# Attention and mixture of experts on one core: the last scatter moved ahead of an adding load, five statistics half a block later, the first output store ahead of a wait

## The reference, cut to what matters

```python
x = x + layernorm(attn(layernorm(x)))            # x is [8, 512, 256] f32: 8 batches of 512 tokens
# the second half, on flat = layernorm(x) as 4096 tokens of 256:
probs = softmax(flat @ gate_W); topk_w, topk_idx = top_k(probs, 2)      # 8 experts, 2 for each token
out = 0.5 * gelu(flat @ shared_W + shared_b)
for e in range(8):
    out = out + combine[:, e:e+1] * (gelu(flat @ W1[e] + b1[e]) @ W2[e] + b2[e])
out = layernorm(out) * gamma + beta              # the inner norm, then gamma and beta
x = x + layernorm(out)                           # the outer norm, then the residual
```

## Time and profile before

| | |
|---|---|
| median of three runs | 739.98 us (738.08 to 740.19) |
| profiled execution | 744.36 us |
| its span in the trace | 742.6 us |
| TensorE matmul busy | 610.8 us, 82% |
| VectorE busy | 447.2 us, 60% |
| ScalarE busy | 448.9 us, 60% |
| GpSimd busy | 278.4 us, 37% |
| mean granted TensorE clock | 0.937 |

### The profile page before, as it was taken

The page is one execution under the profiler, slowest core; times in us unless marked ns, Lnnn a source line. Parts: engine busy times, 40 slices in busy tenths (PEclk is TensorE's granted clock), DMA queues, the critical chain, the costliest instruction groups (busy, mean ns, idle before and its releaser), DMA issues. The chain is left out here.

```text
span 742.6 us, 16982 instructions
## 1 busy us (share of the span) xinstructions
PE 610.8 (82%) x5031; PEld 519.4 (70%) x5031; DVE 447.2 (60%) x1247; ACT 448.9 (60%) x887; POOL 278.4 (37%) x381
## 2 busy tenths in 40 slices
PE   4778887787776898977979989999999999999400
PEld 3667676576665687855858877889989988888300
DVE  4479898898986554422437533344444445768757
ACT  2557756756744665533734765767666654687755
POOL 4000333443437322644762422334334455352131
PEclk9889999999998899988999999999999999999755
DMA  7453654551265221202112311122212149552378
GB/s 256 173 208 128 194 181 133 153 171 58 78 199 180 73 87 58 59 30 59 59 30 59 104 42 59 43 75 86 73 45 60 48 96 195 120 93 53 71 156 169
DMA packets 45272, 78.25 MB, mean 105 GB/s; under 512 B 16962, under 2 KB 30596, under 8 KB 44804
## 3 DMA queue, kind: packets, MB, share of 16 engines
q1 hardware_dynamic: 33204, 47.14, 19.9%
q0 software_dynamic: 11984, 30.03, 17.0%
HBM read 48.17 MB, written 28.98 MB: 104 GB/s over the span
## 5 line engine op out<-in xcount | busy, mean ns | idle before, releaser
L1440 ACT ACTIVATE X<-banks,b1T,tab 128x256 f32<-128x256 f32 (+1 forms) x320 | 152.8, 533 | 156.3 <-PE banks L528 111.3
L526 PE MATMUL banks<-X,W 128*128 128x256 f16 (+1 forms) x640 | 169.1, 267 | 9.2 <-DVE X L1933 8.6
L528 PE MATMUL banks<-X,W 128*128 128x256 f16 (+1 forms) x640 | 169.1, 267 | 3.5 <-issue 3.5
L1926 DVE SCALAR_TENSOR_TENSOR stage<-X,tab,stage 128x512 f16<-128x512 f32 (+1 forms) x160 | 108.0, 695 | 105.5 <-ACT stage L1446 78.1
L527 PE MATMUL banks<-X,W 128*128 128x256 f16 (+1 forms) x640 | 168.6, 266 | 0.6 <-issue 0.4
L526 PE MATMUL banks<-W,stage 128*128 x576 | 160.2, 278 | 9.8 <-issue 6.5
L809 POOL DMA_INDIRECT y_rows<-X,tb x72 | 79.2, 1100 | 233.2 <-DVE X L1950 220.5
L528 PE MATMUL banks<-W,stage 128*128 x576 | 160.3, 278 | 5.5 <-issue 5.4
L527 PE MATMUL banks<-W,stage 128*128 x576 | 160.4, 279 | 5.0 <-issue 4.7
L1446 ACT ACTIVATE stage<-X,tab 128x512 f16<-128x512 f32 (+1 forms) x160 | 106.9, 678 | 10.4 <-ACT X L1440 6.6
L784 POOL DMA_INDIRECT table<-pay,slot_i x64 | 63.7, 996 | 73.9 <-PE banks L969 51.2
(11 more groups left out here) (295 smaller groups left out, 991.5 us busy)
## 6 DMA issues: line engine op xcount, KB each, us to landing
stage<-in_L_ffn_W SPq DMA_DIRECT2D x10, 1024.0 KB
W<-in_L_ffn_W SPq DMA_DIRECT2D x6, 1024.0 KB
X<-in_L_attn_x SPq DMA_DIRECT2D x8, 512.0 KB, 5.3
out<-X SPq DMA_DIRECT2D x8, 512.0 KB
xf_rows<-zone SPq DMA_DIRECT2D x8, 512.0 KB
u_rows<-b2b SPq DMA_DIRECT2D x8, 512.0 KB
X<-y_rows POOLq DMA_DIRECT2D x8, 512.0 KB, 6.2
away<-W SPq DMA_DIRECT2D x1, 2048.0 KB, 7.4
```

The source lines that it names most:

```text
L526: pe.matmul(o, lh, rh, start=first, stop=False)
L528: return pe.matmul(o, ll, rh, start=False, stop=last)
L1440: a.activation(h32[:, m % 2, r * BT:(r + 1) * BT][:, span(j, p)], PS[m][:, r * BT:(r + 1) * BT][:, span(j, p)], ACT.Gelu, bias=b1T[:, bass ...
L1926: v.scalar_tensor_tensor(o[1], src, tab[:, 1, bass.ds(e, 1)], o[0], ALU.mult, ALU.subtract).then_inc(h_low, 1)
```

## The change

Three edits. On GpSimd's list, `add_rows(6, 1)` moves from block 34 to block 35, so that `scatter(35)` stands ahead of it; and `add_out(0)` moves ahead of the wait for `final_in`. On VectorE's list, the inner statistics of batches 0 to 4 move by half a block each: batch 0's from ahead of `result(28)` to behind it, batch 1's from behind `result(28)` to ahead of `result(29)`, batch 2's to behind `result(29)`, batch 3's to ahead of `result(30)`, and batch 4's to behind `result(30)`, ahead of `inner_factors(0)`. Each is the same instructions as before.

```diff
--- before.py
+++ after.py
@@ -876,10 +876,11 @@
                     add_rows(5 + (j - 30) // 4, 0)
                 if j == 31:
                     add_rows(5, 1)
-                if j == 34:
+                if j == 35:
                     add_rows(6, 1)
+            add_out(0)
             g.wait_ge(final_in, 16 * 3)
-            for b in range(B - 1):
+            for b in range(1, B - 1):
                 add_out(b)
 
 
@@ -2047,8 +2048,8 @@
                     later_leaps()
                 if j == 11:
                     later_jumps()
-                if 29 <= j < 32:
-                    inner_stats(2 * (j - 29))
+                if 30 <= j < 32:
+                    inner_stats(2 * (j - 30) + 1)
                 result(j - 1)
                 if j == 9:
                     later_tops()
@@ -2057,8 +2058,8 @@
                     later_blocks()
                 if j == 11:
                     later_experts()
-                if 29 <= j < 31:
-                    inner_stats(2 * (j - 29) + 1)
+                if 29 <= j < 32:
+                    inner_stats(2 * (j - 29))
                 if j == 31:
                     inner_factors(0)
                 if 32 <= j < 36:
```

## The result

Over twenty runs of each kernel, the changed one took a median of 743.68 us (737.92 to 750.21) and the one before 740.69 us (738.08 to 745.06). The ratio, which leaves out two runs of the changed kernel (749.24 and 750.21 us) that lie over 1.5% above its fastest, is 1.004 with a 95% interval of 1.0024 to 1.0056: 1.8 to 4.1 us slower, where no change, with 740.3 us in a range of 737.6 to 742.6, was forecast.

What follows compares the result with a forecast made beforehand. Bound by the root of batches 0 to 4, then batch 6's second adding load; 744.36 - 1.12 (statistics) + 1.48 (plain loads) = 744.72 us profiled, 4.38 above the median, so 740.3 us, range 737.6 to 742.6.

Steps and rivals of the forecast that it cites:

- What bounds the kernel: The root of batches 0 to 4 times the blocks behind it; the tail hangs on batch 6's second adding load.
- The statistics: VectorE, batches 0 to 4: statistics half a block later start the root 1.12 us sooner.
- Split 31: + 2.32: VectorE's list: split 31 follows batch 2's statistics at 634.31 by 2.32 us, at 636.63.
- My lower bound for this term, 0.40 us: VectorE's root: 0.40 us sooner if statistics followed by a split take 3.04 us in both places.
- the statistics bring nothing: Rival: batch 1's to 4's loads, or 3.04 us ahead of both splits, keep the root; 741.5 us, chance 0.08.
- The scatter ahead of the adding load: GpSimd's tail: block 35's scatter fits in the wait until 705.29, costing nothing, with 2.1 us of cover.
- The second adding load is issued at 705.3 as before: GpSimd's tail: batch 6's second adding load keeps its issue time despite the scatter ahead of it.
- Wrong: Sign against the forecast: GpSimd's second adding load is itself issued later, since the scatter held up the first.
- The plain loads beside it: Tail: SyncE's two last_y loads meet batch 6's second adding load, which lands 1.48 us later.
- the upper bound, 2.96 us: Tail: cost to batch 6's second adding load if SyncE's two plain loads go first.
- The early store: GpSimd's tail: add_out(0) goes at about 706.5 instead of 716.56, priced at nothing and winning nothing.
- The sum: Whole kernel: 744.36 - 1.12 + 1.48 = 744.72 us profiled, giving 740.3 us as median.

Runs made afterwards that it cites:

- E5: Statistics of batches 0 to 4 moved, and block 30's register read put ahead of batch 0's statistics, against the kernel before: 734.41 against 736.21 us, ratio 0.9965.
- E3: Only add_out(0) moved ahead of the wait for final_in, against the kernel before: 696.33 against 696.93 us, ratio 1.0000.
- E4: Whole change, with SyncE's last_y loads held until batch 6's second adding load landed, against the kernel before: 697.69 against 696.93 us, ratio 1.0014.
- E8: Whole change, with last_x (512 KB) loaded together with last_y, against the kernel before: 740.91 against 736.21 us, ratio 1.006.
- E6: Of the five statistics only batch 0's moved, behind result(28), tail as before, against the kernel before: 733.77 against 736.21 us, ratio 0.9968.
- E9: Statistics moved, tail as before, register reads of blocks 30 to 35 six blocks earlier, against the kernel before: 691.20 against 696.53 us, ratio 0.9929.
- E10: Changed kernel with half the last scatter, then an extra 128-row gather, ahead of batch 6's second adding load: 6.65 us between its adding loads; no ratio.
- E1: Only the statistics of batches 0 to 4 moved half a block later, against the kernel before: 695.43 against 696.93 us, ratio 0.9981.

## Why the prediction was wrong, point by point

*What bounds the kernel.* Right. The root was the event that passes its shift on to the last but one scatter whole (column B: 48.85 in E5, where the root is 2.2 us sooner), and the tail's chain went through batch 6's second adding load, after which nothing moved. E3 and E4 show that the other candidate, the stores, has no part in it.

*The statistics.* The mechanism was right and a term mis-sized. VectorE's list went as laid out up to `result(29)`: split 30 was forecast 3.04 us behind the load and came at 3.10, `result(29)` at 9.79 and came at 9.85. The step that failed was "Split 31: + 2.32", with its 0.63 us of idle time as in that block before. It was 1.63 us. The DMA engines' share was 1.03 during that idle time and 0.22 during the one before, which is the likely reason but wasn't varied by itself. The 1.0 us missing there is nearly the whole difference between the 1.12 us forecast and the 0.10 found. In E8, where that idle time happened to be 0.59 us, the root came at 23.74, where 23.61 was forecast. The text had named the two idle times and taken one each because no cause was known; a cause was to be had from the code, where each block's first split begins with a register read (E5). My lower bound for this term, 0.40 us, had 3.04 in both places; even that was a little too high. Of the rivals, the third ("the statistics bring nothing", chance 0.08) is what the root bears out. The reason given for the small gain was off too. From batch 0's load to the root, both orders hold the same five statistics, two splits and two results: `result(28)` has left and `result(30)` has come in. So, with the two idle times as before, the new order could win no more than the 1.05 us in which VectorE had stood for batch 3's load, and that is nearly the whole of the 1.12.

*The scatter ahead of the adding load.* "The second adding load is issued at 705.3 as before" is the step that failed first. What it was argued from was true: the scatter's instructions fit in the wait with time to spare, and a scatter behind a load doesn't make it land later. But the row that showed this was a load on which VectorE waits, not GpSimd; that GpSimd itself gets on later with two DMAs in between stood in no row. It cost 1.13 us, and E4 shows it alone (0.93 us there). The sign was named, under "Wrong", but its reason was not the one: the first load isn't held up by the scatter, it lands as before.

*The plain loads beside it.* That they would meet was forecast, with SyncE at 6.4 us behind the first adding load (6.36 found, 701.13 less 694.77). The size was the upper bound, 2.96 us, and not the 1.48 taken: 3.05 found, and E4 shows that it is these loads. The late second adding load may have a part in that. With GpSimd on time it would have been issued ahead of the plain ones; now they had 0.5 us of lead. Whether 1.48 us would have been right with the order that I had expected was not tried. The Trainium skill, page "DMA: Bandwidth & Descriptors", section "Issuing engines are not separate DMA queues", has DMAs of different engines interleave on the same 16 DMA engines, which spoke against this edit, and the trace agrees: 8.45 us instead of 5.41. The Trainium skill, same page, section "Queues, rings and completion order", has each engine take turns between queues packet by packet; equal turns by bytes, the 1.48 us taken, is not what the trace shows, with at most 0.12 MB of the adding load moved while the two plain loads ran.

*The early store.* Right: nothing (E3, E4).

*The sum.* -0.10 + 1.13 + 3.05 = 4.1 us by the trace, against -1.12 + 1.48 = 0.36. A bias in how the bounds were used shows: each term was given bounds, but the point from which the plain loads start relative to the adding load was taken as known, with a lead of 0.6 us for the adding load (705.29 against 705.9) that turned into 0.5 us for the plain ones. The range's upper end took 2.6 us; the measured 740.69 to 743.68 is 3.0, and the median of before itself stood 0.7 us higher over twenty runs than over three.

## What to carry to other kernels

A DMA that is not on the path may still be what holds another one back that is: before a scatter is moved forward, ask who waits for it and whether their transfers now run beside the load that the chain hangs on. Where an engine stands at a wait for something that others don't need, let the others pass, but move only that one; here E6 gained 1.3 us up to the root from batch 0 alone, and the five together 0.1. And look at the unnamed idle times in front of an engine's work: on an engine that bounds a stretch, register reads moved to earlier blocks were worth 4.9 us together with the reordered statistics (E9), more than any edit of the change.

## What the runs showed of the hardware

A read of one word from SBUF into VectorE's register stands as idle time in front of the next instruction. In front of the splits of blocks 30 to 35 it is 0.58 to 0.71 us where the DMA share in it is 0.3 or less, and 1.0 to 1.9 us where the share is 0.99 to 1.14 (1.81 in E6, 1.89 in E10). One read is an exception, with 0.59 us at a share of 1.12 (E8), so the share alone doesn't fix it. The Trainium skill, page "DMA: Bandwidth & Descriptors", section "Latency and other measured facts", gives a floor of some 600 ns for a `tensor_load`, and the trace agrees, with 0.58 us at its shortest.

Where GpSimd waits for batch 6's first adding load, and has issued two further DMAs since, it issues the next one about 1 us later than with none or one in between (6.57 to 6.89 us against 5.58 to 5.81 in column C), be the second 2 KB or 128 KB. With five further ones, the last 5.6 us before, it wasn't late (E1, batch 3). From the issue of an adding load of 512 KB until VectorE goes on it is 5.3 to 5.6 us with no load of SyncE's beside it, whatever stands behind it on its own queue, 8.2 to 8.5 us beside two plain loads of 512 KB, and 9.1 us beside three.
